# First layer of a two-layer cross-attention kernel: another order of transfers at the opening, of the masks, and of a batch's inverse sums

## The reference

```python
# x, kv: (8, 256, 512); 16 heads of depth d = 16, along the channel axis
q = jnp.einsum('oc,bct->bot', Wq, x) + bq[None, :, None]
k = jnp.einsum('oc,bct->bot', Wk, kv) + bk[None, :, None]
v = jnp.einsum('oc,bct->bot', Wv, kv) + bv[None, :, None]
attn = jnp.einsum('bhqd,bhdk->bhqk', q * scale, k)
attn = jnp.where(kv_mask[:, :, None, :], attn, -jnp.inf)
attn = jax.nn.softmax(attn, axis=-1)
mean = jnp.einsum('bhqk,bhkd->bhqd', attn, v)
ex2 = jnp.einsum('bhqk,bhkd->bhqd', attn, v * v)
std = jnp.sqrt(jax.nn.relu(ex2 - mean * mean))
out = (xn * std + mean) * mask     # xn: x with its masked mean taken off, over its standard deviation
```

## Time and profile before

| | |
|---|---|
| runs of the kernel before | 1747.01, 1755.60 and 1757.85 us, median 1755.6 |
| the profiled execution | 1751.12 us |
| its span, first to last instruction | 1749.3 us |
| TensorE busy in the span | 1641.2 us, 94% |
| VectorE, ScalarE, GpSimd busy | 1242.7, 1063.7 and 516.1 us |
| mean granted clock of TensorE | 0.979 of full speed |

### The profile page before, as it was taken

One profiled execution on the slowest core, in us unless ns is written; L12 is line 12 of the kernel. 1 busy time (PEld: TensorE's weight loads), 2 busy tenths in 40 slices (PEclk: granted clock), 3 DMA queues, 4 the chain that ended last, 5 costly groups with the idle time before them and its releaser, 6 DMA issues.

```text
span 1749.3 us, 30873 instructions
## 1 busy us (share of the span) xinstructions
PE 1641.2 (94%) x10589; PEld 1130.0 (65%) x10589; DVE 1242.7 (71%) x2758; ACT 1063.7 (61%) x2351; POOL 516.1 (30%) x795
## 2 busy tenths in 40 slices
PE   5999999999998988999999899999999899999999
PEld 3434334333343346788878678888888688888888
DVE  2676877778787838988999889999999762323222
ACT  1466766757666657778877878788887642111111
POOL 0135455654546523233223233333333220000000
PEclk7899999999999998999999999999999899999999
DMA  5555354553544413222233534333333330000000
GB/s 150 165 156 183 114 152 134 172 163 115 153 126 132 150 47 105 67 74 74 70 93 76 131 98 109 92 91 92 91 92 84 93 109 1 25 0 25 0 25 13
DMA packets 112556, 167.97 MB, mean 96 GB/s; under 512 B 27401, under 2 KB 43145, under 8 KB 112273
## 3 DMA queue, kind: packets, MB, share of 16 engines
q1 hardware_dynamic: 88720, 132.55, 26.1%
q0 software_dynamic: 20992, 29.12, 6.7%
q10 hardware_dynamic: 2688, 4.33, 0.9%
HBM read 72.06 MB, written 34.60 MB: 61 GB/s over the span
## 4 chain that ended last, share of the span: by engine, by line
PE 56%; DVE 21%; ACT 7%; issue 6%; DMA 5%; SPq 4%; POOL 0%; ACTq 0%; DVEq 0%; POOLq 0%
PE ps L533 11%; PE ps L1929 9%; PE ps L1903 7%; DVE at_t L1381 4%; DVE at_t L1386 4%; PE ps L510 4%; PE ps L1252 4%; PE ps L1262 4%; PE ps L519 3%; SPq L342 3%; PE ps L1201 2%; DMA ring<-top 2%; PE ps L1908 2%; PE ps L496 2%; ACT at_prob L1589 2%
## 5 line engine op out<-in xcount | busy, mean ns | idle before, releaser
L607 DVE TENSOR_REDUCE nmax<-ps 128x2 f32<-128x1024 f32 x256 | 310.0, 1221 | 144.1 <-PE ps L510 142.7
L772 ACT ACTIVATE prob<-ps 128x1024 f32<-128x1024 f32 x256 | 261.8, 1023 | 147.3 <-PE ps L519 142.8
L1589 ACT ACTIVATE at_prob<-at_t,at_nmax 128x256 f32<-128x256 f32 x512 | 256.6, 506 | 85.6 <-DVE at_nmax L1386 74.8
L533 PE MATMUL ps<-prob,v 128*64 128x512 f32 x1024 | 280.0, 625 | 2.0
L1386 DVE CUSTOM_DVE_ANT_0 at_t<-at_t,at_off 128x256 f32<-128x256 f32 x512 | 233.5, 492 | 8.8
L1747 POOL TENSOR_TENSOR at_low<-at_low,at_high 128x512 fp32r<-128x512 f32 x64 | 86.7, 1355 | 463.9 <-DVE at_high L1415 463.9
L2088 DVE CAST mlp_h_hi<-mlp_h 128x512 fp32r<-128x512 f32 x64 | 28.4, 444 | 213.0 <-ACT mlp_h L2000 179.9
L2000 ACT ACTIVATE mlp_h<-ps,b 128x512 f32<-128x512 f32 x48 | 33.1, 690 | 218.3 <-PE ps L1903 218.3
L510 PEld LDWEIGHTS ps<-ring 64*128 64x128 f32 x512 | 48.5, 187 | 168.1 <-issue 134.5
L1201 PE MATMUL ps<-ident,at_prob 128*128 128x128 f32 x1024 | 156.9, 276 | 0.0
L1381 DVE SCALAR_TENSOR_TENSOR at_t<-ps,mask_self 128x512 f32<-128x512 f32 x192 | 131.2, 684 | 19.5 <-PE ps L1190 19.0
(11 more groups left out here) (218 smaller groups left out, 3915.5 us busy)
## 6 DMA issues: line engine op xcount, KB each, us to landing
ring<-rows SPq DMA_DIRECT2D x62, 512.0 KB, 5.5
rows<-shares_of SPq DMA_DIRECT2D x90, 256.0 KB
at_k_stack<-at_high SPq DMA_DIRECT2D x256, 64.0 KB, 2.5
at_q_stack<-at_high SPq DMA_DIRECT2D x128, 64.0 KB, 2.7
at_q_stack<-at_high POOLq DMA_DIRECT2D x128, 64.0 KB, 2.5
at_q_stack<-at_low SPq DMA_DIRECT2D x128, 64.0 KB, 2.3
at_k_stack<-at_low POOLq DMA_DIRECT2D x128, 64.0 KB, 2.3
c_in<-in_ctx SPq DMA_DIRECT2D x8, 512.0 KB, 8.5
```

The source lines that it names most:

```text
L533: mm = eng.matmul(ps[2 * QD * k:2 * QD * (k + 1), VB, :], v[:, c, HG * G + 2 * p + k, :], prob[:, M % PROBS, k, :], start=(c == 0), stop=( ...
L607: eng.tensor_reduce(nmax[:, n % 2, j, 2 * p:2 * p + 2], ps[:, at:at + 2, :], AX, ALU.max, negate=True).then_inc(s_max, 1)
L772: eng.activation(prob[:, M % PROBS, :, :], ps[:, ST:ST + 2, :], ACT.Exp, scale=float(HD0) ** -0.5).then_inc(s_exp, 1)
L1589: ins = eng.activation(prob[:, m % 2, i, :], t[:, p, i, :], ACT.Exp, scale=-1.0, bias=nmax[:, m % 4, i:i + 1], accum_out=z[:, T % 2, j, 2 ...
```

## The change

Four things are altered, all of them in `layer0`.

- At the opening, the first transfers of q's rows are issued by ScalarE rather than SyncE; the value weights and their bias are loaded ahead of the second group's rows rather than behind them; the constants are written for one more ring slot first, and for the last two only after the rows of group 1 have been read; the first v item stands in step 5 rather than 4; and the unread matmuls are 11 rather than 21 plus 1 and 1 in the last two steps (the tuple).
- `masks(b+1)` stands at step 0 of w%4 = 2 rather than at step 6 of w%4 = 1, two steps later.
- `shares_out` is split. Its write stays at w%4 = 2 but behind `rows_out("q")`. Its two reads (`shares_back`) move to w%4 = 3, behind `tops_in`.
- What follows from these reads moves too: `mean_squared` from step 4 to 6, `positive_variance` from 0 to 2, `roots` from 2 to 3, `normal_x` from 5 to 6; on GpSimd, at w%4 = 3, the first regroup comes ahead of `finish_shares` and the second ahead of `finish_variance`.

```diff
-        if s == 4 and w == 0:
+        if s == 5 and w == 0:
             return [("v", 0, (0, 1))]
...
         rows_out("k", 0, (0,))
-        rows_out("q", 0, (0,))
         for p in range(2):
             first_rows_in("k", p)
+        for p in range(2):
             first_rows_in("q", p)
-        constants_out(0, scrap, s_const, 1, RING)
-        constants_out(1, far, s_far_out, 1, RING)
+        eng.dma_start(w0[:, :, 2 * S:], d["w0"][:, :, 2 * S:]).then_inc(s_wv, DMA)
+        eng.dma_start(bv0[:], d["bv0"]).then_inc(s_wv, DMA)
+        constants_out(0, scrap, s_const, 1, 2)
+        constants_out(1, far, s_far_out, 1, 2)
         rows_out("k", 0, (1,))
         rows_out("q", 0, (1,))
-        eng.dma_start(w0[:, :, 2 * S:], d["w0"][:, :, 2 * S:]).then_inc(s_wv, DMA)
-        eng.dma_start(bv0[:], d["bv0"]).then_inc(s_wv, DMA)
         rows_in("k", 1)
         rows_in("q", 1)
+        constants_out(0, scrap, s_const, 2, RING)
+        constants_out(1, far, s_far_out, 2, RING)
...
             eng.dma_start(d["shares0"][b % 2].rearrange("h (a e) -> (h a) e", a=P // NH), z[:]).then_inc(s_rd, DMA)
+
+        def shares_back(b):
+
             if b:
                 eng.wait_ge(s_fin, FINISH * (b - 1) + 2)
...
+            if w % NG == 3 and b >= 0 and w < GROUPS:
+                shares_back(b)
...
+            if w % 2 == 0 and ahead < PAIRS:
+                rows_out("q", ahead)
             if w % NG == 2 and b >= 0:
                 shares_out(b)
+            if w == GROUPS + 2:
+                shares_back(b)
             if w % 2 == 0 and ahead < PAIRS:
-                rows_out("q", ahead)
                 rows_out("k", ahead)
...
-                    busy((0, 0, 3, 2, 0, 8, 0, 7, 0, 0, 1, 1)[N], VB, k_rows[:, 0, 0, :])
+                    busy((0, 0, 3, 0, 3, 0, 0, 3, 0, 0, 1, 1)[N], VB, k_rows[:, 0, 0, :])
...
-                if (w, s) == (0, 5):
+                if (w, s) == (0, 6):
                     values(0)
...
-                if w % NG == 0 and 0 <= b - 2 < LAST and s == 0:
+                if w % NG == 0 and 0 <= b - 2 < LAST and s == 2:
                     positive_variance(b - 2)
-                if w % NG == 0 and 0 <= b - 2 < LAST and s == (5 if w < GROUPS else 3):
+                if w % NG == 0 and 0 <= b - 2 < LAST and s == (6 if w < GROUPS else 5):
                     normal_x(b - 2)
...
         high_of("q", 0)
+        taken(eng, "q", 0)
+        for part, at in ((0, 0), (0, 48), (1, 16)):
+            eng.dma_start(d["rows0"][0, 0:1].rearrange("s p (i r) t -> (s p i) r t", r=ROWS)[:, at:at + HD0, :],
+                          shares_of[0:ROWS, 0, part, :].bitcast(F32)).then_inc(s_first_out["q"], DMA)
...
-                if s == 6 and w % NG == 1 and b + 1 < NB:
+                if s == 0 and w % NG == 2 and b + 1 < NB:
                     masks(b + 1)
...
-                if s == 4 and w % NG == 3 and 0 <= b - 1 < LAST:
+                if s == 6 and w % NG == 3 and 0 <= b - 1 < LAST:
                     mean_squared(b - 1)
-                if s == (2 if w < GROUPS else 1) and w % NG == 0 and 0 <= b - 2 < LAST:
+                if s == 3 and w % NG == 0 and 0 <= b - 2 < LAST:
                     roots(b - 2)
...
+            if n >= 0:
+                regroup(eng, 2 * n)
             if w % NG == 3 and 0 <= b - 1 < LAST:
                 finish_shares(b - 1, 0)
                 finish_shares(b - 1, 1)
-            if n >= 0:
-                regroup(eng, 2 * n)
+            if n >= 0 and w % NG == 3:
+                regroup(eng, 2 * n + 1)
             if w % NG == 3 and 0 <= b - 1 < LAST:
                 finish_variance(b - 1)
```

More of the change, by code:

```diff
@@ L348, in constants_written @@
             if name == "q":
-                eng.wait_ge(s_const, 2 * DMA * (2 if n else 1))
+                eng.wait_ge(s_const, 2 * DMA * min(n + 1, 3))
             else:
-                eng.wait_ge(s_far_out, 2 * DMA * (n // NG + (2 if n else 1)))
+                eng.wait_ge(s_far_out, 2 * DMA * (n // NG + min(n + 1, 3)))
         def first_rows_in(name, p):
@@ L643, in squares_of_x @@
             if b == 0 and h == 0:
-                eng.wait_ge(s_const, 4 * DMA)
+                eng.wait_ge(s_const, 6 * DMA)
             eng.tensor_tensor_reduce(scrap[:], X[:, b, h, :], X[:, b, h, :], 1.0, 0.0,
@@ L781, in masks @@
             if b:
-                eng.wait_ge(s_far_out, 2 * DMA * (b + 1))
+                eng.wait_ge(s_far_out, 2 * DMA * (b + 2))
             eng.wait_ge(s_mask, b + 1)
@@ L934, in gpsimd @@
                 squares(2 * b + 1)
-            if n >= 0:
+            if n >= 0 and w % NG < 3:
                 regroup(eng, 2 * n + 1)
```

## The result

The changed kernel took 1759.52 us (median, 1749.32 to 1764.07), the kernel before 1750.69 on the same chip (1745.71 to 1757.85). The ratio is 1.0037, with a 95% interval of 1.0021 to 1.0052. That is 6.5 us slower (the means of the runs differ by 6.5 us, the medians by 8.8), where I had forecast 5.3 faster. By the prediction's own bound of 1% this is "no change", but the sign was wrong, and the interval excludes 1.

The account below looks back on a forecast made before the run. TensorE, busy 94%, was taken to bound the kernel with its gaps. Opening -4.5, tops -12.5, masks -6.5 + 2.8, square +9.8, roots +4 and clock +1.6 gave -5.3 from 1752.9: 1747.6, said as 1747; own range 1740 to 1755, 8-in-10 range 1733 to 1760.

Parts of the forecast that it names:

- bound of 1%: Whole kernel: about 1% (17.5 us) is what a measurement can tell from no change; chance of staying within it 0.8.
- the second layer, which I take as unchanged: Second layer: assumed not to move; the forecast was to count as wrong if it did.
- Wait 1.85 instead of 1.2, 6 times: Roots at w%4 = 0: TensorE waits longer for exp of step 4, +4 us (0 to 6).
- I count 4 falls for 3: Granted clock: one more fall to the lower level behind TensorE's waits, +1.6 us.
- rival 2: Batches: k's rows still hold up the tops, whose waits stay beside the square's and roots'; slower, 1767 us, chance 0.1.
- The tops' waits: w%4 = 3 and the layer's end: TensorE's waits for tops all go, -11.7 and -0.8 us, together -12.5.
- The square's new wait: Behind the late read of `rz`: the square waits for GpSimd's mean, TensorE then 1.4 us, 7 times, +9.8 us.
- who else is behind it: Late read: `finish_variance` ends some 11 us after it, when VectorE and the roots' table load need it; no further wait.
- Rival 1: Late read: `rz` lands within 4.5 us of issue, so the square's wait nearly goes; 1732 us, chance 0.15.
- The opening: Before the first turned scores: rows land 3.5 us sooner and the k product gains 1 more, -4.5 us together.
- 7 times 0.4 is +2.8: Masks in step 0: exp of step 2 ends 0.4 us late each time, +2.8 (0 to 5) against -6.5.
- rival 4: Opening: ScalarE's queue has engines of its own, 4 us more gain, 1743 us, chance 0.05.

Follow-up runs that it names:

- all three trials: Tail's moved steps undone in the changed kernel, added to the kernel before, and added to run 11: 0.33, 0.00 and 0.15%.
- run 11: Changed kernel with clip, roots and `normal_x` back at their old steps everywhere, late read and later square kept: ratio 0.9966 to the kernel before.
- Run 6: Kernel before with only square, clip, roots and `normal_x` moved later inside the batches: ratio 1.0071.
- 12: run 11 with clip, roots and `normal_x` moved at the first layer's tail alone: ratio 0.9981 to the kernel before.
- run 1: Changed kernel with clip, roots and `normal_x` at the tail (w = 32) back at their old steps: ratio 1.0004 to the kernel before.
- run 8: Kernel before with opening and masks, plus shares written and read on SyncE's queue between q's and k's rows: ratio 1.0063.
- run 10: Kernel before with the opening alone, q's first three row transfers left on SyncE's queue: first turned scores at 59.13 us in one execution.
- run 9: Kernel before with opening and masks, one group in four's tops issued by GpSimd ahead of `finish_shares`, square two steps later: ratio 0.9995.
- run 5: Kernel before with the late read and the batches' moved square, clip, roots and `normal_x`; opening, masks and tail as before: ratio 1.0044.

## Why the prediction was wrong, step by step

The ratios make a ladder from the kernel before to the changed one: opening and masks -0.45% (± 0.18), the late read with the square +0.11% (± 0.21), clip, roots and `normal_x` in the batches +0.38% (± 0.23), the same at the tail +0.33% (± 0.25, or 0.16% by all three trials). In us: -7.9, +1.9, +6.7, +5.8, together the 6.5 measured. The prediction had for the same four -8.2, -2.7, +4 and 0, and +1.6 for the clock over all. The second and third rungs are best read together. Between them stands run 11, where the early clip makes waits of its own (12.5 us for the maxima) in the place of the roots', and the prediction knew no such kernel. Its terms for the two come to +2.9 us with the clock, and +8.6 was measured.

**What failed first: "the second layer, which I take as unchanged".** The diff moves the three steps at w = 32 too, and there the prediction's rule for them (each later step costs the difference of two waits) has nothing to do with what is late: `normal_x` feeds X, GpSimd and the second layer's first rows. That link was in the trace of before, where GpSimd's products on X (from 621.00 us) stand directly ahead of its work for the second layer (L1747, at 626.13). The term was put at 0 without a reason. It is 3 us by three trials, and 5.8 by the ladder, in the company of the change.

**The roots: the wait was right, the falls of the clock were undercounted.** "Wait 1.85 instead of 1.2, 6 times" was measured as 1.88, six times. The step "I count 4 falls for 3" failed: 6 in the batches. It also went against the prediction's own rate, 3 falls behind 7 waits of that kind, which rival 2 used and which gives 5 or 6 falls for 13 waits. That the clock is what makes clip, roots and `normal_x` cost 6.7 us in the ladder is likely but not shown. Run 6 speaks for it, with 41.3 us at the lower level for 10.2. But the two profiles of the batches with the steps kept (11, 12) have 6.8 and 17.1 us, the two with the steps moved (after, 1) 20.5 and 17.1, and in the mean the latter take 3.5 us longer, half of the 6.7.

**The read and the tops: a wait that was not in the sum.** The tops' waits in the batches went as forecast, -11.7 us; the one at the layer's end stayed (0.75 us for 0.78), so of -12.5 it is about -11.7. The square's new wait was put at 7 times 1.4, 9.8 us; it is 1.3 to 1.7 in five batches, 0.3 in one and 2.2 at the layer's end, 9.8 us in the sum as well. What failed is the answer to "who else is behind it": the list followed the mean to GpSimd, VectorE and ScalarE and left out what stands behind the read in SyncE's own queue. The ring's rows do, and the scores wait 4.3 us for them. That is about the difference between the forecast -2.7 and the rung's +1.9 (-1.8 to +5.6 us, which leaves out -2.7); since run 11 has other waits, the agreement of the two sizes is partly chance. The read itself was little slower than forecast: 6.9 us to GpSimd in the mean of the six batches, and 6.1 in run 1 with the same batches, for 5.7 to 6.4. The two rows of before were of a read with nothing large just ahead of it. Rival 1, the read there in 4.5 us, did not occur.

**The opening was mis-sized, the masks were better.** I had 4.5 us. The first links came true: the last row landed at 37.86 us for 41.35, 3.5 sooner (though no run shows the 1.5 us that the sum takes "to arrive"), and the k product 4.5 us sooner (45.92 for 50.39). But the second half's rows and tops then took longer (the transfer of the tops 4.88 us for 4.12), and the first turned scores gained 3.0. Even this was partly the luck of the profile: the first exp comes 1.2 to 3.9 us sooner in the eight profiles with the whole opening (2.6 in the mean), and 0 to 1.8 us sooner in the five with the old one (1.0), so the opening gives about 1.6 us, and alone it measured -0.05% (± 0.17). The masks' "7 times 0.4 is +2.8" is 0: no wait stands there, and the masks alone gave -5.6 us for my -3.7. That the two terms together hit their sum, -7.9 for -8.2, is luck.

**Right for the reason given:** the tops' waits go, because k's rows leave ahead of the maxima (run 8); ScalarE's queue brings nothing and k's first rows land later (rival 4, run 10); GpSimd is what the square waits for, with ScalarE idle 2.9 to 5.0 us ahead of it; the roots' wait. Rival 2 had the right sign for other reasons: its condition, tops still late, did not occur.

## What to carry to other kernels

A step table that serves two phases is costed twice: find who waits for a moved step in the last iteration, where there is no next group to cover it. Of a wait, price what follows it as well, but count falls of the clock over several profiles: the same batches had two in one profile and four in another. Of a transfer that moves, list what stands behind it in its own queue. And when a bundle moves the time little, run its parts: here two of four gave 0.45% and the rest took more than that back, so the fastest kernel measured is the change without its largest part (0.9955; run 11, which keeps the late read at 0.9966, can't be told from it).

## What the runs showed of the hardware that I had not expected

A small DMA lands late when large ones stand just ahead of it. The 32 KB write of the shares landed a median of 1.5 us after its issue with nothing large just ahead and 6.1 us behind q's three rows of 256 KB; in run 8 SyncE issued nothing for 5.8 us because of it. Four transfers of 4 KB each from GpSimd's queue (run 9) fared no better beside SyncE's rows.

The granted clock did not follow the length of a wait alone. The nine waits of 2.1 to 2.4 us for the maxima in runs 11 and 12 were accompanied by a fall three times. Of the roots' waits of 1.9 us it was five of six in the run with the steps alone, five of six in run 5, four of six in run 1 and three of six in the changed kernel. What sets them apart was not tried.
